# Exponents of two bounds read straight from PSUM, and the next batch's x work placed over more steps, in an attention and feed-forward kernel

## The reference

```
for lvl in range(4):
    x = query[:, ::2**lvl, :]
    outs.append(_mha(x, in_proj_w[lvl], in_proj_b[lvl], out_w[lvl], out_b[lvl]))
current = outs[-1]
for lvl in (2, 1, 0):
    current = _upsample_linear(current, outs[lvl].shape[1]) @ up_w[lvl].T + up_b[lvl] + outs[lvl]
x = _layernorm(query + current)
x = _layernorm(x + _L0_ffn_ref(x, ...))
```

## Time and profile before

| | |
|---|---|
| median of 3 runs | 3830.7 us (3830.51 to 3838.46) |
| the profiled execution, its own time | 3840.0 us |
| its span, first to last instruction | 3838.2 us |
| PE busy | 3552.8 us, 93% |
| DVE busy | 2577.4 us, 67% |
| ACT busy | 2605.9 us, 68% |
| POOL busy | 1134.4 us, 30% |
| mean granted TensorE clock | 0.962 of full speed |

### The profile page before, as it was taken

The page is one execution under the profiler, slowest core; times in us unless marked ns, Lnnn a source line. Parts: engine busy times, 40 slices in busy tenths (PEclk is TensorE's granted clock), DMA queues, the critical chain, the costliest instruction groups (busy, mean ns, idle before and its releaser), DMA issues. The chain is left out here.

```text
span 3838.2 us, 59302 instructions
## 1 busy us (share of the span) xinstructions
PE 3552.8 (93%) x20995; PEld 1429.2 (37%) x20995; DVE 2577.4 (67%) x4836; ACT 2605.9 (68%) x3266; POOL 1134.4 (30%) x1060
## 2 busy tenths in 40 slices
PE   5899999989989989989999998959999999999998
PEld 3333233333333333333333332224445444444444
DVE  5787988888887898898798889833333333333333
ACT  2788778878878878878878888834444444444443
POOL 2243453454364363354344444220000000000000
PEclk7999989989999999999998999979999999999999
DMA  4533323332342332242333233210000000000000
GB/s 145 156 94 91 104 86 94 95 108 81 95 124 72 94 119 83 87 130 72 96 104 103 86 98 102 61 53 4 20 12 12 12 23 12 12 12 15 20 12 12
DMA packets 227902, 269.85 MB, mean 70 GB/s; under 512 B 51268, under 2 KB 187524, under 8 KB 226976
## 3 DMA queue, kind: packets, MB, share of 16 engines
q1 hardware_dynamic: 218352, 257.09, 22.5%
q10 hardware_dynamic: 9216, 8.39, 0.6%
HBM read 159.75 MB, written 101.45 MB: 68 GB/s over the span
## 5 line engine op out<-in xcount | busy, mean ns | idle before, releaser
L957 ACT ACTIVATE a_probs<-a_p_s,a_unit_now 128x1024 f32<-128x1024 f32 x1360 | 1441.5, 1109 | 312.4 <-PE a_p_s L1280 308.6
L1061 DVE TENSOR_REDUCE a_part_max<-a_p_r 128x1 f32<-128x512 f32 x2048 | 1304.0, 676 | 257.8 <-PE a_p_r L1293 254.2
L1293 PE MATMUL a_p_r<-a_k_st,a_q_st 48*128 48x512 f16 (+2 forms) x2944 | 915.2, 381 | 147.9 <-DVE a_part_max L1061 75.0
L1652 PE MATMUL p_h<-f_h_hi,f_w_hi 128*128 128x512 f16 x2048 | 776.7, 379 | 3.2 <-issue 3.2
L1652 PE MATMUL p_h<-f_h_lo,f_w_hi 128*128 128x512 f16 x2048 | 776.2, 379 | 0.0
L1310 PE MATMUL a_p_o<-a_probs,a_v_aug 128*17 128x512 f32 (+2 forms) x5888 | 743.8, 585 | 2.3 <-ACT a_raw L967 2.3
L1280 PE MATMUL a_p_s<-a_q_st,a_k_st 50*128 50x512 f16 (+2 forms) x2944 | 693.3, 375 | 32.9 <-ACT a_probs L957 32.8
L1293 PEld LDWEIGHTS a_p_r<-a_k_st,a_q_st 48*128 48x128 f16 x2944 | 222.0, 94 | 1176.9 <-DVE a_part_max L1061 799.3
L1514 ACT ACTIVATE f_h_f<-p_h,f_sc_now 128x512 f32<-128x512 f32 x256 | 175.9, 687 | 517.2 <-PE p_h L1652 515.2
L1061 DVE TENSOR_REDUCE a_row_max<-a_p_r 128x1 f32<-128x512 f32 (+2 forms) x672 | 426.4, 675 | 84.1 <-PE a_p_r L1293 82.3
L1461 POOL TENSOR_TENSOR f_rstd<-f_var_eps,f_minus_half 128x1 f32<-128x1 f32 x64 | 36.4, 568 | 1240.4 <-DVE f_var_eps L1607 1240.4
(11 more groups left out here) (157 smaller groups left out, 4657.1 us busy)
## 6 DMA issues: line engine op xcount, KB each, us to landing
qk_scratch<-a_qk_room SPq DMA_DIRECT2D x288, 128.0 KB
a_w_lo<-wqkv_inner SPq DMA_DIRECT2D x30, 768.0 KB, 4.5
a_a_lo<-a_attn SPq DMA_DIRECT2D x448, 32.0 KB, 2.0
a_q_st<-qk_scratch SPq DMA_DIRECT2D x64, 192.0 KB, 3.5
a_k_st<-qk_scratch SPq DMA_DIRECT2D x64, 192.0 KB, 4.4
a_o_lo<-wo_inner SPq DMA_DIRECT2D x24, 512.0 KB, 3.5
a_qk_room<-wf SPq DMA_DIRECT2D x23, 512.0 KB, 3.8
a_q_st<-qk_scratch SPq DMA_DIRECT2D x112, 96.0 KB, 2.2
```

What stands on the lines that cost most here:

```text
L957: act.activation(probs[:, s % 2, 2 * p:2 * p + 2, :], p_s[:, 2 * p:2 * p + 2, :], ACT.Exp, scale=unit_now[:, lvl:lvl + 1]).then_inc(exp_do ...
L1061: dve.reduce_max(out, src, AX.X).then_inc(max_read.sem, 1)
L1293: ins = pe.matmul(p_a[:, r * size:(r + 1) * size], q_st[rows_of(j, ROWS), query_at:query_at + 128], k_st[rows_of(j, ROWS), key_at:key_at + ...
L1652: ins = pe.matmul(out, a, c, start=first and n == 0, stop=last and n == len(terms) - 1)
```

## The change

It does two things.

1. The factor `TOP` (a power of two) moves into the matrix of ones (`pool.memset(ones, TOP)`), and the lower limit `FLOOR` into `b_top` (one more DVE instruction in the opening). So the two columns in PSUM are the bound itself, `bound` and its instruction go, and the two exponent instructions read PSUM as integers. The bank is free when both are done (`span_set`), not after the first.
2. In the placement for batches 1 to 7 (not for the opening, `first`) the x work and the projections move. `xcut` 0 and 1 go from steps 24.3 and 24.8 to 24.5 and 26.0; `wcut` of level 2 from 25.3 to 27.3; the four spans from 25.9, 26.3, 26.7, 27.1 to 27.5, 28.3, 29.1, 29.9; `proj` 0 and 1 from 27.85 and 29.85 to 30.85 and 32.85; `v` 0 from 28.85 to 34.85. What follows moves too: `wcut` of level 1 from 34.15 to 39.15, of level 3 from 47.15 to 53.15, of level 0 from 57.15 to 61.15; `proj` 2 and `v` 1 from 36.85 and 37.85 to 42.85 and 43.85; the last, `proj` 14, from 76.85 to 80.85. Times and numbers of all other tasks stay.

```
-            side.update(places([(("proj", n), load_at[lvl] + 6 + gap[lvl] * i) for i, n in enumerate(mine)], taken, 2))
-            side.update(places([(("v", n), (6 if lvl == 0 else load_at[lvl] + 7) + (4 if lvl == 0 else 2) * kt) for n, kt in turns], taken))
+            side.update(places([(("proj", n), load_at[lvl] + (9 if lvl == 2 else 6) + gap[lvl] * i) for i, n in enumerate(mine)], taken, 2))
+            side.update(places([(("v", n), (6 if lvl == 0 else load_at[lvl] + (10 if lvl == 2 else 7)) + (4 if lvl == 0 else 2) * kt) for n, kt in turns], taken))
...
-    p += [(load_at[2] + 3 + (6 if first else .5) * n, "xcut", n) for n in range(2)]
+    p += [(load_at[2] + 3.2 + (6 if first else 1.5) * n, "xcut", n) for n in range(2)]
...
-        cut_at = (load_at[lvl] + proj_at[lvl]) / 2 + 1
+        cut_at = (load_at[lvl] + proj_at[lvl]) / 2 + (1 if first or lvl != 2 else 3)
...
-        span_at = cut_at + .3 if first else load_at[2] + 4.6 + .4 * n
+        span_at = cut_at + .3 if first else load_at[2] + 6.2 + .8 * n
...
-                pool.memset(ones[:, :], 1.0).then_inc(ones_set.sem, 1)
+                pool.memset(ones[:, :], TOP).then_inc(ones_set.sem, 1)
...
+                dve.wait_ge(b_top_done.sem, 1)
+                dve.tensor_scalar(b_top[:, :, :], b_top[:, :, :], FLOOR / TOP / 128, None, ALU.max).then_inc(b_top_done.sem, 1)
...
-                            dve.tensor_scalar(bound[:, :], p_a[:, 0:2], TOP, FLOOR, ALU.mult, ALU.max).then_inc(span_read.sem, 1)
-                            dve.wait_ge(span_read.sem, span_read.value(it, n + 1))
-                            dve.tensor_scalar(unit_qk[:, :].bitcast(I32), bound[:, :].bitcast(I32), EXPONENT, None, ALU.bitwise_and)
-                            dve.tensor_scalar(scale_qk[:, lvl, :].bitcast(I32), bound[:, :].bitcast(I32), EXPONENT, EXPONENT, ALU.bitwise_xor, ALU.bitwise_and)\
+                            bound = p_a[:, 0:2].bitcast(I32)
+                            dve.tensor_scalar(unit_qk[:, :].bitcast(I32), bound, EXPONENT, None, ALU.bitwise_and)
+                            dve.tensor_scalar(scale_qk[:, lvl, :].bitcast(I32), bound, EXPONENT, EXPONENT, ALU.bitwise_xor, ALU.bitwise_and)\
...
-                pe.wait_ge(b_top_done.sem, 1)
+                pe.wait_ge(b_top_done.sem, 2)
...
-                            {"max": max_read, "proj": qk_read, "neg": neg_read, "v": v_done, "mid": mid_read, "lift": lift_read, "row": row_read, "span": span_read,
+                            {"max": max_read, "proj": qk_read, "neg": neg_read, "v": v_done, "mid": mid_read, "lift": lift_read, "row": row_read, "span": span_set,
```

More of the change, by code:

```diff
@@ L449, in attention @@
         reach, ones = sb("reach", [128, 2, 2, 2], BF16), sb("ones", [128, 128], BF16)
-        bound, unit_qk, scale_qk = sb("bound", [128, 2]), sb("unit_qk", [128, 2]), sb("scale_qk", [128, LEVELS, 2])
+        unit_qk, scale_qk = sb("unit_qk", [128, 2]), sb("scale_qk", [128, LEVELS, 2])
         col_qk, unit_next, unit_now = sb("col_qk", [128, LEVELS, 4]), sb("unit_next", [128, LEVELS]), sb("unit_now", [128, LEVELS])
@@ L492, in attention @@
         ones_set, b_top_done, w_top_done, x_top_done = sig("ones_set", 0), sig("b_top_done", 0), sig("w_top_done", 0), sig("x_top_done", 2)
-        reach_done, span_mm, span_read = sig("reach_done", 4), sig("span_mm", 4), sig("span_read", 4)
+        reach_done, span_mm = sig("reach_done", 4), sig("span_mm", 4)
         span_set, col_set, unit_set, unit_taken = sig("span_set", 4), sig("col_set", 4), sig("unit_set", 4), sig("unit_taken", 2)
```

## The result

The changed kernel takes 3841.4 us (median of 13 runs, 3833.1 to 3852.3), against 3831.7 us before in the same session (3830.5 to 3841.8): a ratio of 1.0019, 95% interval 1.001 to 1.0027. It is slightly slower, where 18.4 us less were forecast. Its profiled execution took 3838.4 us, with a span of 3835.4.

The account below looks back on a forecast made before the run. PE, busy 93% of the span, was taken as the bound, with DVE or ACT holding it up in places. -4.2 - 0.1 + 2.1 = -2.2 us a batch, times 7, opening -3: -18.4, giving 3812, range 3786 to 3834.

Parts of the forecast that it names:

- Exponents from PSUM, 0.16 us each: The two exponent instructions reading PSUM take about 0.16 us each, whatever POOL does; a PSUM surcharge could add up to 4 us.
- The lock costs its length, 3.3 us a batch: Steps 25 to 27: L1085 hanging on POOL's work costs its length less 0.17, 3.3 us a batch, which goes.
- The 26.0: Steps 24 to 29 after the change: 22.5 + 1.5 + 2.7, less something for the reading; 4.2 us less than 30.2.
- Opening, 3 us: Opening: two PE waits behind locked L1085, 3.21 and 3.16 us, shrink; 3 us gained, bounds 0 and 6.4.
- Steps 24 to 29, the wait for `reach`, 1.5 us: Steps 24 to 29: PE waits for POOL's reach behind w_lo and o_lo, 1.5 us a batch, bounds 0 and 4.
- The clock, half of 13.6 us: Steps 24 to 29: half the present 13.6 us at low clock stays, as lock and doubled x_top go; costs 2.7 us.
- ACT's floor, 22.5 less 0.7 for the reading: Steps 24 to 29: ACT's busy time, 22.5 us or below, since the reading of proj 0 leaves too.
- Steps 30 to 37, -0.1: Steps 30 to 37: a third piece costs 0.8, the level 1 wcut and its low clock leave; 28.7 us, 0.1 less.
- Steps 38 to 83, +2.1: Steps 38 to 83: two more pieces, 16 for 14, cost 1.6 to 2.6 us a batch; taken as +2.1.
- The rival that two of the `w` cuts cost the clock in every batch: Steps 38 to 83 grow by 5.4 us a batch from two low-clock spells; total 3850 us; chance 0.13.
- the sum of the forecast (3812.3): Whole kernel: -2.2 us a batch for 7 batches, opening -3, together -18.4; from the median 3830.7 to 3812.
- The rival "eaten up": Steps 24 to 29 keep 13.6 us at low clock and the reach wait: 28.5 us there, 3830 in total; chance 0.17.

Follow-up runs that it names:

- e1: The kernel before with only the exponents read from PSUM, all x work at its old steps: 3821.0 us, ratio 0.9969.
- e2: The kernel before with only the placement moved, exponents still from the clamped SBUF copy: 3840.2 us, ratio 1.0017.
- e11: The changed kernel with the first w_lo and first o_lo moved behind the last span on POOL alone: 3826.5 us, ratio 0.9976.
- e5: e4 with o_lo two steps later in POOL's order (offset for ocut 2.4 instead of .4): 3799.7 us, ratio 0.9906.
- e4: The changed kernel with only the first w cut put back two steps, to 25.3 instead of 27.3: 3814.6 us, ratio 0.9954.
- e10: e1 with an offset of 2.2 steps for the first wcut on POOL, putting w_lo behind all reach: 3857.1 us, ratio 1.0061.
- e3: The changed kernel with the four spans earlier, at steps 26.5 to 27.4 instead of 27.5 to 29.9: 3824.7 us, ratio 0.9975.
- e9: e5 with the exponents taken from the clamped SBUF copy again: 3809.1 us, ratio 0.9942.

## Why the prediction was wrong

- **Exponents from PSUM, 0.16 us each: right.** 154 and 148 ns, and no lock. The surcharge for a PSUM source that the Trainium skill gives (VectorE: DVE Perf Modes, TRN2 errata) does not show at this size: 154 ns from PSUM, 158 from SBUF.
- **The lock costs its length, 3.3 us a batch: wrong.** It was priced from DVE's row and not from PE's. e1 gained 1.1 a batch; the wait that PE shows behind the long lock is 1.06 us. In the new order it costs nothing that shows: steps 24 to 29 take 30.0 in e2 and in the changed kernel. The 26.0 itself is added up from ACT's floor and does not contain the lock. The error lies in the reading of the kernel before, where 3.3 us of lock had to explain a part of the 31.0, and in one of the two reasons for halving the low clock.
- **Opening, 3 us: low.** It gave 4.9 (e1 5.0), within the bounds of 0 and 6.4.
- **Steps 24 to 29, the wait for `reach`, 1.5 us: the step that failed.** The prediction named `w_lo` and `o_lo` between the first and the third `reach`, 5.8 us of POOL work, and still took 1.5, with a bound of 4, without a reason for what would hide the rest. (It also put the first span matmuls at 27.85, where the change has 27.5.) Measured: 5.3 a batch. In batch 2 PE waits 5.12 of those 5.77 us. It is ready for its second span at 817.8, when `w_lo` has run for 0.3 us; in the kernel before it came there at 817.78, 1.3 us after `w_lo` had ended. How much of this is the later `w` cut and how much the projections taken from PE was not measured apart. e11, which mends POOL's order alone, brings the wait to 0.7 and the stretch to 26.7.
- **The clock, half of 13.6 us: wrong.** 0.69 over 30.1 us is 18.7 us at half clock, 7.5 us of time at 0.40, and not 2.7. The second spell begins in the 3.73 us wait, but e11 has almost as much low clock without that wait, so what brings it is open. In e5 the clock is between 0.70 and 0.92.
- **ACT's floor, 22.5 less 0.7 for the reading: high.** ACT is busy 20.3 us in the mean of the seven batches. 20.3 + 5.3 + 7.5 = 33.1 against 30.0 measured: the terms overlap by 3, as they did in batch 6 before. This is why the 26.3 of e4 is no proof of the forecast's 26.0: there the floor is 20.2, the wait 2.1 and the low clock 14.4 us long (5.8 at 0.40), so that misses of both signs meet near the same sum.
- **Steps 30 to 37, -0.1: low.** They take 27.7 instead of 28.7. The forecast put 0.8 for a third piece on the 27.8 of full-clock batches; the third piece shows no cost here, where a `w` cut has left as well. The profile of before had in addition the low clock of the earlier trace rows in its batches 1 to 3, e1's only in one, so 28.8 was high as a mean.
- **Steps 38 to 83, +2.1: right within 1.** +2.8 in the change, of which 0.8 is the clock in step 55 of two batches; +2.1 in e4. The rival that two of the `w` cuts cost the clock in every batch did not come true: one spell follows the `w` cut of step 53, in two batches of seven.
- **The sum.** 3841.4 is 29.1 us above the sum of the forecast (3812.3). Of these 16.8 lie in the profiles, which differ by -1.6 us where -18.4 was forecast: steps 24 to 29 account for 27.7 (7 x 4.0) and steps 38 to 83 for about 5, while the opening gives 2 back and steps 30 to 37 and 0 to 23 about 7 each. The other 12.3 come from the step from the profile to the median: the forecast took 9.3 off, as in the kernel before, and the changed kernel's profile is 3.0 below its median. The rival "eaten up" described best what happened, at 3830, and it too counted the lock as gained.
- **The spread of the runs goes with the clock.** Of the 13 runs of the changed kernel the shortest, 3833.1 us, has a mean granted clock of 0.962, the longest, 3852.3, has 0.955. 0.007 of 3838 us is 54 us at the lower level, for 19.2 us of time, 0.36 each. The median run has 0.959, both profiles have 0.962 and 0.961. By the 0.40 of the prediction the 0.003 are an estimated 9 us, as much as the medians lie apart (the kernel before has 0.962 in the median of the 26 runs beside e1). Where in a median run these spells lie no trace shows.

## What to carry to other kernels

Price a stalled instruction by the wait it causes on the engine that sets the end, not by its own length, and ask what else on that path waits for the same cause: here, in the new order, the freed lock uncovered a wait for a result of 0.2 us behind the very same POOL instruction (e2 against the changed kernel). When a consumer is moved, write down, for each of its occurrences, what stands in front of its producer on the producer's own queue; a producer that hands over several small results with 3.4 us and 2.4 us of other work between them stalls its reader once per gap. Taking work off the bound engine can make such waits longer, since it arrives earlier (argued here, not measured by itself). And a gap closed by moving the big work behind the small is only closed if the next reader of the big work has moved as well (e10 against e11 and e5).

## What was unexpected of the hardware

- The lower clock kept to its places. Two executions of the changed kernel have it in the same steps of the same batches (13.7 us from step 27 in batches 0 to 6, 6.8 us in step 55 of batches 0 and 2 only) and differ in the opening and in a few steps of batch 0, although every batch has the same work; other kernels with the same tasks in step 55 have it in batches 0 and 1 (e3, with 2 in part), 5 (e4), 2 and 4 (e5), 2 and 3 (e9) or none (e2, e11). PE's work just before does not tell them apart: it is busy 5.53 of the 6.4 us before the fall in batch 2, and 5.43 of 6.3 at the same place in batch 1, where the clock stays. What selects the batch is open.
- A fall of the clock was seen with PE at work as well as with PE standing still: in step 55 it comes in the middle of 24 matmuls in a row that began at 917.85 (from 919.5 on one takes 0.42 us and not 0.28), and in the changed kernel's step 27 within a wait of 3.73 us.
- The lock is exact: L1085 from SBUF ends at 816.46 where POOL's `w_lo` ends at 816.44, even for two elements a partition, and the same operation with its source in PSUM never showed it in the kernels that use it (148 to 158 ns mean). That agrees with the Trainium skill (SBUF — State Buffer, who interferes with whom), which has the engine that comes second block for the whole of the other's instruction when VectorE is in a two-port mode. Whether L1085 was in such a mode no run here shows.
